# First attention layer: the scores of a pair of blocks in one call over four banks

## The chip, the cores and the metric

One core of one Trainium2 chip. The metric is device time in microseconds (us) of the whole kernel, the median of several runs.

## The reference, cut to what matters

```python
x = x + attn_a(layernorm(x))   # 16 heads of 8, blocks of 64 tokens, softmax inside a block
x = x + ffn(layernorm(x))      # top 2 of 8 experts
x = x + attn_b(layernorm(x))
x = x + ffn(layernorm(x))
# attn_a, per block of 64 tokens:
scores = einsum('bnihd,bnjhd->bnhij', q, k) / sqrt(8)
out = einsum('bnhij,bnjhd->bnihd', softmax(scores), v)
```

x has 16 rows of 256 tokens with 128 features, so 4096 tokens. Only the score step of attn_a is changed.

## The kernel before

The kernel runs six stages one after the other: setup, first layer, experts, second layer, experts, combine. In the first layer (`first_layer`) a tile is 128 tokens, a pair is two tiles (16 pairs), and a batch or quad, c, is four tiles (8 quads). Every engine runs its own written-out program over a common turn number p; semaphores counted by name tie them. A turn p of TensorE (PE) does: scores of pair p+1, the weighted sum over values of pair p-1 (`mixing`), transposes of the probabilities of pair p (`turn`), and the transpose back of pair p-1 (`flip`). Between them stand, in even turns, the projections K and Q of the next quad, the router's ranks and a transpose for the router (`turn_x2`); in odd turns the router's logits, the projection V and the transpose of the quad after next (`turn_x`).

The scores of a pair have two halves, gp 0 and 1. Half gp lies in `psS[gp]`, two PSUM banks of 512 columns. Within a half, `score(p, gp)` issues eight matmuls with 32 rows of K (one group of heads, g) and 64 columns of tokens, on tiles of the array given by `tile_position`. Matmuls in f32 leave two records each in the trace.

VectorE (DVE) does for each half `peak` (maximum over keys, L710) and `shift` (subtract it, L717, which writes `prob`), with `divide(p-2)` (L725, L729) between the two halves, and then in even turns the router's weights, places and statistics (from L791), in odd turns the router's choice (L737 to L767) and statistics. ScalarE (ACT) does `rise_up` (exponential, L880), `out_flat` (copies of the transposed probabilities, L886), `out_side` (L892), `out_k` (four copies, L857), `out_q` (L850), `out_v` (L867), the normalisation (L836) and, up to turn 6, the rounding of expert weights (`weight_high`, L900). GpSimd (POOL) adds the residual and sends rows to the experts' regions by indirect DMA (L479).

The waits that matter: `score(p, gp)` waits for `shifted` of the same half of pair p-1, since it overwrites it; `mixing(p-1)` waits for `divided` of pair p-2; `project_q` waits for `k_out`, since Q and K pass through one bank; `out_q(c)` waits for all scores that read the old `qT`; `project_v(c)` waits for `q_out` or, from the fourth quad on, for `taken`.

Of the kernel before, what the change touches and what calls it, by code (L numbers as in the profile page):

```python
# [330 lines left out]
def counted(k, tag, *names):  # L331

    return [k.sem(f"{tag}_{x}") for x in names]


def first_layer(k, d):

    nc = k.nc
    tag = "la"
    BLK = 64  # L340
# [3 lines left out]
    scored, peaked, shifted, risen, flat, flat_copied, mixed, mixed_copied, flipped, inverted, divided, based, summed = counted(  # L344
        k, tag, "scored", "peaked", "shifted", "risen", "flat", "flat_copied", "mixed", "mixed_copied", "flipped",
        "inverted", "divided", "based", "summed")
# [9 lines left out]
    psS = k.wide[0:2]  # L356
    psP, psO, psX = k.bank[4:6], k.bank[6], k.bank[7]
    with ExitStack() as ctx:
# [8 lines left out]
        xT, qT = two("xT", [P, TB]), sb("qT", [P, TB])  # L367
        kz = two("kz", [P, 4, TB])
# [137 lines left out]
        def _(pe):  # L506
# [10 lines left out]
            def project_k(c):  # L517
                pe.wait_ge(copied, c + 1)
                if c >= 4:
                    pe.wait_ge(spotted, c - 3)  # L520
                elif c >= 1:
                    pe.wait_ge(v_out, c)
                nc.tensor.matmul(psX[:, :], k.wqk[0][:, 1, :], xT[c % 2][:, :], start=True, stop=True).then_inc(k_ready, 1)

            def project_q(c):
                pe.wait_ge(k_out, c + 1)
                nc.tensor.matmul(psX[:, :], k.wqk[0][:, 0, :], xT[c % 2][:, :], start=True, stop=True).then_inc(q_ready, 1)

            def project_v(c):

                if c >= 3:
                    pe.wait_ge(taken, c - 2)
                else:
                    pe.wait_ge(q_out, c + 1)
                for tb in range(2 * BATCH):
                    for cls in range(2):
                        last = nc.tensor.matmul(
                            psX[BLK * cls:BLK * (cls + 1), tb * 64:(tb + 1) * 64], xT[c % 2][:, tb * BLK:(tb + 1) * BLK],
                            k.wv[0][:, cls * 64:(cls + 1) * 64], start=True, stop=True, tile_position=(0, BLK * cls))
                last.then_inc(v_ready, 1)  # L540
# [19 lines left out]
            def route_ranks(c):  # L560

                u = c % 2
                pe.wait_ge(picked, c + 1)
                if c + 3 < QUADS:
                    pe.wait_ge(v_out, c + 4)
                out = psX[:, 0:BATCH * EXPERTS].rearrange("p (t e) -> p t e", e=EXPERTS)
                wide = [P, BATCH, EXPERTS]
                nc.tensor.matmul(out, k.ones[:, :], k.region[:, :].unsqueeze(1).to_broadcast(wide), start=True, stop=False)
                nc.tensor.matmul(out, k.ones[:, :], both[u][:, BATCH, :].unsqueeze(1).to_broadcast(wide), start=False, stop=False)
                for t in range(BATCH - 1):  # L570
                    many = BATCH - 1 - t
                    nc.tensor.matmul(out[:, t + 1:, :], k.ones[:, :], both[u][:, t, :].unsqueeze(1).to_broadcast([P, many, EXPERTS]),
                                     start=False, stop=False)
                nc.tensor.matmul(out, k.upper[:, :], both[u][:, 0:BATCH, :], start=False, stop=True).then_inc(ranked, 1)

            def score(p, gp):
                c = p // 2
                if gp == 0 and p % 2 == 0:
                    pe.wait_ge(q_out, c + 1)
                if p >= 1:  # L580
                    pe.wait_ge(shifted, 2 * (p - 1) + gp + 1)
                for t in range(2):
                    for b in range(2):
                        at = slice((p % 2 * 2 + t) * P + b * BLK, (p % 2 * 2 + t) * P + (b + 1) * BLK)
                        for g2 in range(2):
                            g = 2 * gp + g2
                            last = nc.tensor.matmul(  # L587
                                psS[gp][BLK * b:BLK * (b + 1), g2 * 512 + t * 256:g2 * 512 + (t + 1) * 256],
                                qT[32 * g:32 * (g + 1), at], kz[c % 2][32 * g:32 * (g + 1), :, at],
                                start=True, stop=True, tile_position=(32 * g, BLK * b))  # L590
                last.then_inc(scored, 1)

            def turn(p, gp, w):
# [17 lines left out]
            def mixing(p):  # L611

                c = p // 2
                pe.wait_ge(flat_copied, 4 * p + 4)
                pe.wait_ge(v_out, c + 1)
                if p >= 1:
                    pe.wait_ge(divided, p)
                for t in range(2):
                    for gp in range(2):
                        for b in range(2):  # L620
                            for i in range(4):
                                col = t * 256 + gp * P + b * BLK
                                last = nc.tensor.matmul(
                                    psO[32 * i:32 * i + 2 * (HD + 1), col:col + BLK],
                                    stand[c % 2][:, p % 2 * 2 + t, b, 4 * gp + i, :],
                                    probT[p % 2][gp][t][:, i * P + b * BLK:i * P + (b + 1) * BLK], start=True, stop=True,
                                    tile_position=(0, 32 * i))
                last.then_inc(mixed, 1)

            def flip(p):  # L630
                pe.wait_ge(mixed_copied, p + 1)
                for x in range(4):
                    last = nc.tensor.transpose(psO[:, x * P:(x + 1) * P], side[:, x * P:(x + 1) * P], k.ident)
                last.then_inc(flipped, 1)

            for p in range(-3, 2 * QUADS + 6):
                c = p // 2
                even = p % 2 == 0
                here, ahead, behind = 0 <= p < PAIRS, 0 <= p + 1 < PAIRS, 0 <= p - 1 < PAIRS
                if ahead:  # L640
                    score(p + 1, 0)
                if even and 0 <= c - 3 < QUADS:
                    route_ranks(c - 3)
                if behind:
                    mixing(p - 1)
                if even and 0 <= c + 1 < QUADS:
                    project_k(c + 1)
                if not even and 0 <= c - 2 < QUADS:
                    route_logits(c - 2)
                if here:  # L650
                    turn(p, 0, 0)
                    turn(p, 0, 1)
                if ahead:
                    score(p + 1, 1)
                if behind:
                    flip(p - 1)
                if even and 0 <= c + 1 < QUADS:
                    project_q(c + 1)
                if not even and 0 <= c + 1 < QUADS:
                    project_v(c + 1)  # L660
                if here:
                    turn(p, 1, 0)
                    turn(p, 1, 1)
                if even and 0 <= c - 2 < QUADS:
                    turn_x2(c - 2)
                if not even and 0 <= c + 2 < QUADS:
                    turn_x(c + 2)
# [5 lines left out]
        def _(dve):  # L673
# [3 lines left out]
            for u in range(2):  # L677
                for cls in range(2):
                    last = nc.vector.memset(stand[u][BLK * cls:BLK * (cls + 1), :, :, :, cls * (HD + 1) + HD], 1.0)
# [26 lines left out]
                last.then_inc(moments2, 1)  # L706

            def peak(p, gp):
                dve.wait_ge(scored, 2 * p + gp + 1)
                nc.vector.tensor_reduce(most[gp][:, :], psS[gp][:, :].rearrange("p (h k) -> p h k", k=BLK), X, ALU.max)\  # L710
                    .then_inc(peaked, 1)

# [85 lines left out]
            for p in range(-4, 2 * QUADS + 6):  # L798
                c = p // 2
# [27 lines left out]
        def _(act):  # L827
# [18 lines left out]
            def out_q(c):  # L846
                act.wait_ge(q_ready, c + 1)
                if c >= 1:
                    act.wait_ge(scored, 4 * c)
                nc.scalar.activation(qT[:, :], psX, ACT.Identity, bias=k.cols[:, 0:1]).then_inc(q_out, 1)  # L850

            def out_k(c):
                act.wait_ge(k_ready, c + 1)
                if c >= 2:
                    act.wait_ge(scored, 4 * (c - 1))
                for j in range(4):
                    last = nc.scalar.activation(kz[c % 2][:, j, :], psX, ACT.Identity, bias=k.kbias[0][:, j:j + 1],  # L857
                                                scale=k.const[:, C_HEAD + j:C_HEAD + j + 1])
                last.then_inc(k_out, 1)
# [43 lines left out]
            for p in range(-4, 2 * QUADS + 6):  # L903
                c = p // 2
# [1039 lines left out]
```

## Time and profile before

| | |
|---|---|
| median of 3 runs | 886.98 us (883.74 to 887.29) |
| span of the profiled execution | 926.2 us |
| PE busy | 746.1 us, 81% |
| DVE busy | 505.9 us, 55% |
| ACT busy | 524.2 us, 57% |
| POOL busy | 363.0 us, 39% |
| mean granted TensorE clock | 0.902 |

The profiled execution is known by its span alone; it is 39 us longer than the median of the runs. The first layer fills the stretch from about 20 to 258 us. "Busy" counts an engine's own instructions; PE records of matmuls side by side overlap, so a busy PE is not a full array.

### The profile page before, as it was taken

What the parts mean: (1) busy time and instruction counts of PE and PEld (TensorE: products, weight loads), DVE (VectorE), ACT (ScalarE), POOL (GpSimd) and SP (SyncE); (2) the same over time, 40 slices, a digit from 0 to 9 for tenths busy, and PEclk for the clock granted to TensorE, in tenths of its full rate; (3) what the DMA queues carried; (4) which work ended last, traced back from release to release, by engine and by line L of the source; (5) the groups of instructions that cost most, each with busy time, mean ns of one, the idle gap of its engine ahead of it and who ended that gap; (6) DMA issues with size and microseconds to landing.
All of it is one profiled execution on the core that took longest, in us unless ns stands there. A gap on an engine that the chain in (4) does not pass through costs nothing. (4 is left out here: it accounts for less than half of the span.)

```text
span 926.2 us, 27043 instructions
## 1 busy us (share of the span) xinstructions
PE 746.1 (81%) x8818; PEld 600.2 (65%) x8819; DVE 505.9 (55%) x1787; ACT 524.2 (57%) x1016; POOL 363.0 (39%) x446
## 2 busy tenths in 40 slices
PE   1688887786179999999967898877629999999970
PEld 1356655455158888888834677666518888888860
DVE  3366876653435555555527565454435555555534
ACT  0589975652056666666617986643116666666630
POOL 0454764536713333333333114447642333333330
PEclk9989987885589999999999997997659999999985
DMA  6134011011211111111135000111121111111117
GB/s 193 38 98 121 22 40 36 25 31 56 75 39 48 46 46 46 49 49 46 38 107 172 11 4 24 30 33 41 40 72 40 48 49 47 46 46 46 49 33 268
DMA packets 53546, 54.45 MB, mean 59 GB/s; under 512 B 8192, under 2 KB 43008, under 8 KB 53472
## 3 DMA queue, kind: packets, MB, share of 16 engines
q1 hardware_dynamic: 41024, 31.61, 12.2%
q0 software_dynamic: 8640, 18.11, 6.0%
q10 hardware_dynamic: 3808, 3.70, 1.2%
q8 instruction: 53, 0.87, 0.4%
q14 instruction: 21, 0.17, 0.1%
HBM read 29.51 MB, written 23.86 MB: 58 GB/s over the span
## 5 line engine op out<-in xcount | busy, mean ns | idle before, releaser
L1656 POOL DMA_INDIRECT expert_out<-moe_b_out,moe_b_place x71 | 68.0, 957 | 145.3 <-DVE moe_b_out L1812 145.3
L1656 POOL DMA_INDIRECT expert_out<-moe_a_out,moe_a_place x71 | 68.0, 958 | 145.1 <-DVE moe_a_out L1812 145.1
L1688 PE MATMUL wide<-wgu,moe_b_hi 128*128 x284 | 94.9, 415 | 0.0
L1688 PE MATMUL wide<-wgu,moe_a_hi 128*128 x284 | 94.3, 413 | 0.0
L1069 POOL DMA_INDIRECT routed<-stream,lb_place x64 | 62.3, 974 | 63.1 <-PE wide L1117 18.5
L479 POOL DMA_INDIRECT routed<-stream,la_place x64 | 63.2, 987 | 42.9 <-DVE la_place L784 26.2
L1704 PE MATMUL wide<-wd,moe_a_hidT 128*128 x568 | 75.5, 276 | 1.4 <-DVE moe_a_out L1812 0.7
L1704 PE MATMUL wide<-wd,moe_b_hidT 128*128 x568 | 75.4, 276 | 1.3 <-DVE moe_b_out L1812 0.7
L1704 PEld LDWEIGHTS wide<-wd,moe_b_hidT 128*128 128x128 f32 x568 | 69.0, 192 | 2.2 <-issue 2.2
L1704 PEld LDWEIGHTS wide<-wd,moe_a_hidT 128*128 128x128 f32 x568 | 69.0, 192 | 2.2 <-issue 2.0
L1763 ACT ACTIVATE moe_b_glow<-wide 128x512 f32<-128x512 f32 x71 | 42.6, 599 | 44.1 <-PE wide L1688 44.0
L1763 ACT ACTIVATE moe_a_glow<-wide 128x512 f32<-128x512 f32 x71 | 42.5, 598 | 43.5 <-PE wide L1688 43.5
L1824 DVE TENSOR_TENSOR moe_b_hid<-wide,moe_b_glow 128x512 f32<-128x512 f32 x71 | 49.1, 692 | 20.7 <-PE wide L1688 9.2
L1824 DVE TENSOR_TENSOR moe_a_hid<-wide,moe_a_glow 128x512 f32<-128x512 f32 x71 | 49.1, 692 | 19.8 <-PE wide L1688 8.7
L1688 PE MATMUL wide<-wgu,moe_b_lo 128*128 x142 | 56.3, 396 | 0.0
L1688 PE MATMUL wide<-wgu,moe_a_lo 128*128 x142 | 56.0, 394 | 0.0
L1688 PEld LDWEIGHTS wide<-wgu,moe_b_hi 128*128 128x128 f32 x284 | 48.4, 190 | 6.9 <-issue 0.3
L1688 PEld LDWEIGHTS wide<-wgu,moe_a_hi 128*128 128x128 f32 x284 | 48.2, 190 | 6.5 <-issue 0.3
L1770 ACT ACTIVATE moe_b_hidT<-wide 128x512 f32<-128x512 f32 x71 | 42.4, 597 | 12.7 <-PE wide L1696 12.7
L1770 ACT ACTIVATE moe_a_hidT<-wide 128x512 f32<-128x512 f32 x71 | 42.4, 597 | 12.7 <-PE wide L1696 12.7
L710 DVE TENSOR_REDUCE la_most<-wide 128x16 f32<-128x1024 f32 x32 | 38.7, 1210 | 19.0 <-PE wide L587 18.9
L1812 DVE TENSOR_SCALAR moe_a_out<-wide,moe_a_weight 128x128 f32<-128x128 f32 x71 | 24.9, 351 | 39.4 <-PE wide L1704 39.4
(282 smaller groups left out, 1778.3 us busy)
## 6 DMA issues: line engine op xcount, KB each, us to landing
moe_a_rows<-routed SPq DMA_DIRECT2D x71, 67.0 KB
moe_b_rows<-routed SPq DMA_DIRECT2D x71, 67.0 KB
lb_outs<-expert_out SPq DMA_DIRECT2D x8, 512.0 KB
la_stage<-in_wg SPq DMA_DIRECT2D x8, 256.0 KB, 2.6
la_stage<-in_wu SPq DMA_DIRECT2D x8, 256.0 KB, 3.2
wd<-in_wd SPq DMA_DIRECT2D x8, 256.0 KB, 3.8
kept<-stream SPq DMA_DIRECT2D x8, 256.0 KB
lb_kept<-kept SPq DMA_DIRECT2D x8, 256.0 KB
```

The lines of the kernel that those rows point to most:

```text
L479: pool.indirect_dma_start(d.routed[:, :], bass.IndirectOffsetOnAxis(ap=place[:, t, j:j + 1], axis=0), k.stream[:, t, :], None).then_inc(se ...
L710: nc.vector.tensor_reduce(most[gp][:, :], psS[gp][:, :].rearrange("p (h k) -> p h k", k=BLK), X, ALU.max)\
L1069: pool.indirect_dma_start(d.routed[:, :], bass.IndirectOffsetOnAxis(ap=place[:, t, j:j + 1], axis=0), k.stream[:, t, :], None).then_inc(se ...
L1656: pool.indirect_dma_start(d.expert[:, :], bass.IndirectOffsetOnAxis(ap=place[s % 4][:, 0:1], axis=0), out[u][:, :], None).then_inc(stored[ ...
L1688: last = nc.tensor.matmul(ps[u][:, :], x[u][:, :], w(j, part), start=i == 0, stop=i == 2)
L1704: last = nc.tensor.matmul(psY[:, 0:D], hidT[u][:, c * P:(c + 1) * P], k.wd[:, bass.ds(e, 1), c, :].rearrange("p a c -> p (a c)"), start=c ...
L1763: nc.scalar.activation(glow[s % 2][:, :], psG[s % 2][:, :], ACT.Silu).then_inc(glowing.sem, 1)
L1770: nc.scalar.activation(hidT[u][:, :], psH[:, :], ACT.Copy).then_inc(crossed_copied.sem, 1)
L1812: nc.vector.tensor_scalar(out[u][:, :], psY[:, 0:D], weight[s % 4][:, 0:1], None, ALU.mult).then_inc(out_ready.sem, 1)
L1824: nc.vector.tensor_tensor(hid[u][:, :], psU[u][:, :], glow[u][:, :], ALU.mult).then_inc(hidden.sem, 1)
```

## The change

`score(p)` makes both halves at once: per tile and per 64 tokens it issues the four groups of heads one after the other, over both `psS[0]` and `psS[1]`. It waits for the second `shift` of pair p-1, signals `scored` once, and stands at one place in the turn: behind `flip` and the projection of Q or V, ahead of the second pair of `turn` calls. Before, half 0 stood at the head of the turn and half 1 ahead of `flip`. The waits on `scored` in `peak`, `out_q` and `out_k` are counted anew.

```diff
-            def score(p, gp):
+            def score(p):
                 c = p // 2
-                if gp == 0 and p % 2 == 0:
+                if p % 2 == 0:
                     pe.wait_ge(q_out, c + 1)
                 if p >= 1:
-                    pe.wait_ge(shifted, 2 * (p - 1) + gp + 1)
+                    pe.wait_ge(shifted, 2 * p)
                 for t in range(2):
                     for b in range(2):
...
-                        for g2 in range(2):
-                            g = 2 * gp + g2
-                            last = nc.tensor.matmul(
-                                psS[gp][BLK * b:BLK * (b + 1), g2 * 512 + t * 256:g2 * 512 + (t + 1) * 256],
+                        for g in range(4):
+                            col = g % 2 * 512 + t * 256
+                            last = nc.tensor.matmul(psS[g // 2][BLK * b:BLK * (b + 1), col:col + 256],
...
                 last.then_inc(scored, 1)
...
-                if ahead:
-                    score(p + 1, 0)
                 if even and 0 <= c - 3 < QUADS:
                     route_ranks(c - 3)
...
-                if ahead:
-                    score(p + 1, 1)
                 if behind:
                     flip(p - 1)
                 if even and 0 <= c + 1 < QUADS:
                     project_q(c + 1)
                 if not even and 0 <= c + 1 < QUADS:
                     project_v(c + 1)
+                if ahead:
+                    score(p + 1)
                 if here:
                     turn(p, 1, 0)
                     turn(p, 1, 1)
...
             def peak(p, gp):
-                dve.wait_ge(scored, 2 * p + gp + 1)
+                dve.wait_ge(scored, p + 1)
...
-                    act.wait_ge(scored, 4 * c)            # out_q
+                    act.wait_ge(scored, 2 * c)
...
-                    act.wait_ge(scored, 4 * (c - 1))      # out_k
+                    act.wait_ge(scored, 2 * (c - 1))
```

## Rows read from the trace of the kernel before

**Rows 1.** The page: span and busy time of the engines.
```profile
span 926.2 us, 27043 instructions
PE 746.1 (81%) x8818; PEld 600.2 (65%) x8819; DVE 505.9 (55%) x1787; ACT 524.2 (57%) x1016; POOL 363.0 (39%) x446
```

**Rows 2.** Busy time by stretch: length, PE, PEld, DVE, ACT, POOL, clock, DMA share, GB/s.
```profile
60.90:79.10 18.20, 15.36 (x273) 10.27 (x273) 13.53 (x30) 17.64 (x31) 9.87 (x14) 1.00 0.22 62
79.10:98.40 19.30, 16.73 (x285) 11.54 (x285) 12.27 (x43) 18.27 (x32) 8.50 (x14) 1.00 0.45 125
...
89.60:109.20 19.60, 17.03 (x294) 11.78 (x294) 15.28 (x51) 18.37 (x32) 10.12 (x13) 1.00 0.12 35
109.20:212.20 103.00, 81.87 (x1212) 55.83 (x1211) 65.70 (x194) 62.38 (x104) 56.52 (x76) 0.85 0.11 36
...
45.70:49.20 3.50, 1.18 (x6) 0.30 (x2) 3.43 (x4) 3.50 (x7) 3.42 (x4) 0.88 0.00 1
```

**Rows 3.** Timeline of PE: start, length, line, count, idle before and its releaser.
```profile
61.48 1.09 PE L587 MATMUL wide<-la_kz,la_qT 32*64 32x256 f32 x16
...
94.58 0.66 PE L633 MATMUL wide<-const,la_side 128*128 128x128 f32 x4
95.16 1.15 PE L537 MATMUL wide<-wv_a,la_xT 128*64 128x64 f32 x32
...
98.98 1.09 PE L587 MATMUL wide<-la_kz,la_qT 32*64 32x256 f32 x16
...
100.25 1.09 PE L623 MATMUL wide<-la_probT,la_stand 128*18 128x64 f32 x64
101.27 1.12 PE L523 MATMUL wide<-la_xT,wqk_a 128*128 128x512 f32 x2
102.23 1.04 PE L608 MATMUL wide<-const,la_prob 128*128 128x128 f32 x8
...
105.27 1.12 PE L527 MATMUL wide<-la_xT,wqk_a 128*128 128x512 f32 x2 [0.39 <-ACT la_kz L857]
...
109.18 1.09 PE L587 MATMUL wide<-la_kz,la_qT 32*64 32x256 f32 x16
```

**Rows 4.** Timeline of ACT, the same columns, 90 to 105 us.
```profile
90.20 1.05 ACT L880 ACTIVATE la_prob<-la_prob 128x1024 f32<-128x1024 f32 x1
...
92.68 1.14 ACT L900 ACTIVATE wgu<-la_stage 128x512 fp32r<-128x512 f32 x2
93.72 0.58 ACT L892 ACTIVATE la_side<-wide 128x512 f32<-128x512 f32 x1
...
102.43 2.78 ACT L857 ACTIVATE la_kz<-wide,kbias_a,const 128x512 f32<-128x512 f32 x4 [0.21 <-PE wide L523]
```

**Rows 5.** Timeline of DVE, the same columns, 62 to 100 us.
```profile
62.64 1.23 DVE L710 TENSOR_REDUCE la_most<-wide 128x16 f32<-128x1024 f32 x1 [0.45 <-PE wide L587]
...
92.73 0.19 DVE L737 TENSOR_TENSOR la_logit<-wide,stream 128x32 f32<-128x32 f32 x1 [4.20 <-PE wide L556]
...
96.48 1.19 DVE L710 TENSOR_REDUCE la_most<-wide 128x16 f32<-128x1024 f32 x1
97.70 1.23 DVE L717 TENSOR_TENSOR la_prob<-wide,la_most 128x1024 f32<-128x1024 f32 x1
98.84 0.35 DVE L725 RECIPROCAL la_inv<-wide 128x32 f32<-128x32 f32 x1
99.22 0.42 DVE L729 TENSOR_TENSOR la_mix<-wide,la_inv 128x256 f32<-128x256 f32 x1
```

**Rows 6.** Timeline of PE in the second layer: one of its score calls.
```profile
590.75 1.13 PE L1181 MATMUL wide<-lb_kz,lb_qT 32*32 32x128 f32 x64
```

**Rows 7.** Timelines of PE and ACT in the slower stretch, 120 to 144 us.
```profile
120.12 1.98 PE L587 MATMUL wide<-la_kz,la_qT 32*64 32x256 f32 x16
...
133.11 1.09 PE L587 MATMUL wide<-la_kz,la_qT 32*64 32x256 f32 x16
...
143.55 1.27 ACT L867 ACTIVATE la_stand<-wide 64x512 f32<-64x512 f32 x2 [4.78 <-remote]
```

More of the change, by code:

```diff
@@ L584, in score @@
                         at = slice((p % 2 * 2 + t) * P + b * BLK, (p % 2 * 2 + t) * P + (b + 1) * BLK)
-                        for g2 in range(2):
-                            g = 2 * gp + g2
-                            last = nc.tensor.matmul(
-                                psS[gp][BLK * b:BLK * (b + 1), g2 * 512 + t * 256:g2 * 512 + (t + 1) * 256],
-                                qT[32 * g:32 * (g + 1), at], kz[c % 2][32 * g:32 * (g + 1), :, at],
-                                start=True, stop=True, tile_position=(32 * g, BLK * b))
+                        for g in range(4):
+                            col = g % 2 * 512 + t * 256
+                            last = nc.tensor.matmul(psS[g // 2][BLK * b:BLK * (b + 1), col:col + 256],
+                                                    qT[32 * g:32 * (g + 1), at], kz[c % 2][32 * g:32 * (g + 1), :, at],
+                                                    start=True, stop=True, tile_position=(32 * g, BLK * b))
                 last.then_inc(scored, 1)
```

## The prediction

> **What bounds the kernel now.** I read the page first, to see that no engine is full over the whole span: PE is busy 81%, ACT 57%, DVE 55% [rows 1]. The change touches the first layer alone, so I went to the busy times by stretch. There the reader is to see that two regimes exist. From 60.9 to 109.2 us the TensorE clock is granted in full, and one batch of four blocks (two pairs, an even and an odd turn of the loop) takes 18.2 us without routing, 19.3 when routing begins and 19.6 with all of it. PE works 15.4 to 17.0 us of that, ACT 17.6 to 18.4, DVE 12 to 15 [rows 2]. Nobody idles much, and nobody is full: the period is a chain of hand-overs between engines, with PE and ACT both close to it. From 109.2 to 212.2 the same work takes 103 us at a mean clock of 0.85 [rows 2]; that is four more batches and part of a fifth, some 26 us each.
>
> Third, PE's timeline. In an even turn it starts the next pair's first half of scores at 98.98, mixing at 100.25, K at 101.27, Q only at 105.27 (idle 0.39, for ACT), and the next odd turn starts at 109.18: 10.20 us [rows 3]. Fourth and fifth, the timelines of ACT and DVE, for the durations and hand-overs below [rows 4, 5].
>
> **What the old order gives.** The scores of a pair lie in two halves, psS[0] and psS[1]. PE makes half 0 of pair p+1 at the head of turn p, and half 1 in its middle, each released by its own subtraction on DVE. So DVE works on half 0 of the next pair long before PE comes to that pair's turn, and the division of pair p-2, which DVE does after that half, is done when PE reaches mixing(p-1), which waits for it: DVE starts its division at 98.84 and the product at 99.22, PE mixes at 100.25 after other work [rows 3, 5].
>
> **What the change removes.** A call for one half is eight matmuls of 256 columns, in 16 records; two calls make a pair. A call's records span 1.09 us at full clock, of which the next work overlaps some 0.07: it holds PE 1.02 [rows 3]. The new call has 16 matmuls, 32 records. The trace has no such call, so I bound it: below 1.09, as if eight matmuls ran side by side at the price of four; above 2.04, two old calls. The nearest row is the second layer's scores, L1181, where 64 records of 128 columns on eight tiles take 1.13 us: twice the column-records of an old half in the same time [rows 6]. I take 1.05. The saving is 1 us of PE per pair, 16 us over 16 pairs, if PE were alone.
>
> The Trainium skill, "TensorE: Matmul & The Clock Gate", section "The mechanism" of its part on packing, says that a weight load overlaps running matmuls only where its row group differs. The loads of the second half-block share all four row groups with running matmuls; by that rule a call would cost near 2.04. The row of L1181, where four column groups share each row group, speaks against it.
>
> **What it adds.** Three things. The whole score(p+1) now waits for the second subtraction of pair p; it stands behind mixing, K or router logits, turn(p,0), flip and Q or V on PE; and DVE's first maximum of pair p+1 waits for it. So the head start is gone, and DVE and PE are tied into a loop once per turn. I walk that loop from the start of the first maximum of a pair to that of the next.
>
> Even turn. Maximum 1.22, subtraction to the division's start 1.14 (96.48 to 98.84 is 2.36), reciprocal 0.38, product 0.42, hand-over 0.06 (K copies end at 105.21, Q starts 105.27): mixing starts at 3.22. Mixing 1.02 (100.25 to 101.27); K to its copies 1.16 (101.27 to 102.43); copies to Q 2.84 (102.43 to 105.27); Q holds PE 0.96 (as K, 101.27 to 102.23); score to DVE's start 1.16 (61.48 to 62.64) [rows 3, 4, 5]. Sum 3.22 + 1.02 + 1.16 + 2.84 + 0.96 + 1.16 = 10.36 us. The second subtraction ends at about 5.5, hidden. DVE's own work (5.52 and some 2 of weighing and statistics) is hidden too.
>
> Odd turn, while ACT still rounds weights (turns up to 6). The subtraction ends 1.22 + 1.23 + 0.06 = 2.51; ACT does the exponential, four normalisations and two weight copies in 3.52 (90.20 to 93.72); side copy and hand-over 0.64; flip 0.58 (94.58 to 95.16); V 1.15; score to DVE 1.16 [rows 3, 4, 5]: 9.56 us. Without weights ACT gives back 1.04 (92.68 to 93.72) and the chain is 8.52, but DVE then sets the end: 2.36 + 0.80 + 2.36 for both halves and the division, and 3.75 for routing and statistics (92.73 to 96.48): 9.27 us [rows 4, 5]. V's own wait for the routed logits is inside that.
>
> Side effects at no cost: out_q(c+1) now waits for the score behind Q (before, both halves were issued ahead of it). ACT gets to it at the end of its second exponential anyway, about 10.1, and the score ends at 10.4; behind it stand two copies of turned probabilities, which need PE's turns after that score. They end at about 12.1 of the even turn and the next mixing is due at 13.6: 1.5 of slack. The copy for the router behind them ends near the next exponential's due time, so that cover is thin; if it goes, 0.5 us per batch. No DMA moves; POOL's residual keeps its place behind the division.
>
> **The sum.** Batches of two turns, new against old: turns 2 and 3, 10.36 + 9.56 = 19.92 against 18.2, +1.7; turns 4 and 5, 19.92 against 19.3, +0.6; turns 6 on, 10.36 + 9.27 = 19.63 against 19.6, nothing, for five batches [rows 2]. At the start V(0) now stands ahead of score(0): 1.15 later, less a little caught up; +1.0. Together +3.3, say 3.5 with rounding of hand-overs. The tail (turns 15 on) has no scores, and POOL's row writes follow the routing, which shifts with it.
>
> The profiled execution spans 926.2 us, 39 more than the median 886.98. In it V of turn 9 should take 1.15 us, but ACT gets its result at 143.55 after 4.8 us idle [rows 7], and the clock falls afterwards. I take these stalls to be mostly absent from the timed runs: four to five batches at 26 instead of 19.6 are about the 39. So against the profile's own time: 926.2 + 3.5 = 929.7; against the median 886.98 + 3.5 = 890.5. About 0.5% (4.4 us) is what a measurement can tell from no change.
>
> **Rivals.**
> - *The clock falls more often* (0.2). In an even turn PE, once flip is done at about 6.9, waits for K's copies until 8.26: 1.4 us idle, and about 1.2 before mixing. For it: the stretch 45.7 to 49.2, with PE busy 1.18 of 3.5 and the clock still 0.88, is where it goes to half [rows 2]. Against it: here PE would be busy some 7.3 of 10.4 us. Price: at half clock a score call takes 1.98 instead of 1.09 [rows 3, 7]; mixing, K, Q and score on the chain cost 3.5 more per even turn. Eight times 3 is +24: 914; if half of them, 902.
> - *PE is what counts, and it is faster* (0.16). In the slow regime two calls of 1.98 stand on PE's path, and the old even turn from 120.12 to 133.11 takes 13.0 us [rows 7]. With mixing and K at half clock (about 1.9 and 2.1) and the rest at full, my chain is 3.22 + 1.9 + 2.1 + 2.84 + 0.96 + 1.16 = 12.2, so 0.8 less, and odd turns with the stall save the like. If the timed runs have these stretches, four or five batches give back 1.7 each, 8 in all, and a stall avoided 3.7: 887 + 3.5 - 8 - 3.7 = 879. It decides from three slow batches on. Against it: the 39 us.
> - *The eight don't run side by side* (0.06), the call costs 2.04: +1.0 in each of 15 turns: 905.5. This is also the case in which the change does not do what it says.
> - *Thin covers go* (0.11): the router copy, V's wait, ACT behind out_q: 0.5 to 1 us per batch, 894 to 898.
> - *My forecast* (0.47): 890.5, own range 886 to 895.
>
> **How the numbers follow.** The likeliest is 890.5. The range takes most of both rivals on the slow side up to 905 and the faster one down to 880. Slower by over 0.5% (above 891.4): the clock 0.2, no side by side 0.06, thin covers 0.09 and 0.1 of my own case, 0.45. Faster (below 882.5) 0.15. Within: 0.40.
>
> **What would show it.** After: L587 calls of x32 with about 1.1 us; DVE idle before the first maximum of odd turns, 2 to 3 us, released by PE L587 (about none before); L623 waiting for DVE's product (L727 in the new numbering, L729 now) in nearly every turn, where it did so in few; Q waiting about 1.4 us for ACT's K copies; the batch at 60 to 80 us 19.9 instead of 18.2. Wrong if DVE has no such idle time, or if PEclk has more low slices than before.

## The result, and the profile after

The changed kernel takes 893.59 us (median of 15 runs, 888.58 to 905.65), the kernel before 886.64 beside it (15 runs). The ratio is 1.0085, with a 95% interval of 1.0061 to 1.0109: 7.5 us slower, 5.4 to 9.7 (the medians differ by 7.0). The forecast was 890.5, 3.5 slower: the time lies in the forecast range, the loss is twice the one forecast.

The profiled execution of the changed kernel took 890.17 us, so it can be read against its own runs. The one of before that stands ahead of the prediction cannot: its stalls, some 39 us of late results and low clock, are missing here. The page, with the tenths of busy time and of clock in 40 slices, and the group of DVE's first-layer maxima, last the same group of the kernel before:

```profile
span 887.9 us, 27043 instructions
PE 704.6 (79%) x8818; PEld 578.7 (65%) x8819; DVE 503.4 (57%) x1787; ACT 525.5 (59%) x1016; POOL 363.5 (41%) x446
...
PE   1466677774199999999977889997269999999960
...
PEclk9989999986599999999998999997579999999995
...
L708 DVE TENSOR_REDUCE la_most<-wide 128x16 f32<-128x1024 f32 x32 | 39.1, 1220 | 57.6 <-PE wide L588 57.5
```

```profile
L710 DVE TENSOR_REDUCE la_most<-wide 128x16 f32<-128x1024 f32 x32 | 38.7, 1210 | 19.0 <-PE wide L587 18.9
```

DVE works as much as before (503.4 against 505.9 us [rows 1]) and now idles 57.6 us ahead of its 32 maxima, all but 0.1 of it for the score call; before it was 19.0. That is the lost head start. Lines of the new kernel: score L588, mixing L623, K L523, Q L527, V L537, turned probabilities L608.

Timeline of PE: the end of an odd turn that still has the expert weights on ACT, an even turn, and the mixings that close the next odd one (start, length, line, count, idle before and its releaser), to be laid beside [rows 3]:

```profile
65.01 1.09 PE L623 MATMUL wide<-la_probT,la_stand 128*18 128x64 f32 x64 [1.47 <-DVE la_mix L727]
...
79.00 0.66 PE L633 MATMUL wide<-const,la_side 128*128 128x128 f32 x4 [1.22 <-ACT la_side L890]
79.59 1.15 PE L537 MATMUL wide<-wv_a,la_xT 128*64 128x64 f32 x32
80.67 1.12 PE L588 MATMUL wide<-la_kz,la_qT 32*64 32x256 f32 x32
...
85.25 1.09 PE L623 MATMUL wide<-la_probT,la_stand 128*18 128x64 f32 x64 [1.47 <-DVE la_mix L727]
86.27 1.13 PE L523 MATMUL wide<-la_xT,wqk_a 128*128 128x512 f32 x2
...
88.10 0.60 PE L633 MATMUL wide<-const,la_side 128*128 128x128 f32 x4
90.27 1.12 PE L527 MATMUL wide<-la_xT,wqk_a 128*128 128x512 f32 x2 [1.57 <-ACT la_kz L855]
91.33 1.12 PE L588 MATMUL wide<-la_kz,la_qT 32*64 32x256 f32 x32
92.38 1.09 PE L608 MATMUL wide<-const,la_prob 128*128 128x128 f32 x8
...
95.91 1.09 PE L623 MATMUL wide<-la_probT,la_stand 128*18 128x64 f32 x64 [1.34 <-DVE la_mix L727]
...
105.50 1.09 PE L623 MATMUL wide<-la_probT,la_stand 128*18 128x64 f32 x64 [1.32 <-DVE la_mix L727]
```

Timelines of DVE and ACT over the same two turns, beside [rows 4, 5]:

```profile
72.31 1.23 DVE L708 TENSOR_REDUCE la_most<-wide 128x16 f32<-128x1024 f32 x1 [3.87 <-PE wide L588]
...
81.90 1.23 DVE L708 TENSOR_REDUCE la_most<-wide 128x16 f32<-128x1024 f32 x1 [2.80 <-PE wide L588]
...
84.68 0.42 DVE L727 TENSOR_TENSOR la_mix<-wide,la_inv 128x256 f32<-128x256 f32 x1
...
92.55 1.22 DVE L708 TENSOR_REDUCE la_most<-wide 128x16 f32<-128x1024 f32 x1 [3.87 <-PE wide L588]
```

```profile
74.83 1.06 ACT L878 ACTIVATE la_prob<-la_prob 128x1024 f32<-128x1024 f32 x1 [0.80 <-DVE la_prob L715]
...
78.38 0.57 ACT L890 ACTIVATE la_side<-wide 128x512 f32<-128x512 f32 x1
...
87.43 2.79 ACT L855 ACTIVATE la_kz<-wide,kbias_a,const 128x512 f32<-128x512 f32 x4 [0.43 <-PE wide L523]
```

The loop of the even turn can be read off: first maximum 81.90, product 84.68, mixing 85.25, K 86.27, copies 87.43, Q 90.27, score 91.33, next first maximum 92.55. Every step comes behind the one named ahead of it, four times on another engine. It took 10.65 us. The loop of the odd turn before it took 9.59: first maximum 72.31, exponential 74.83, side copy 78.38, flip 79.00, V 79.59, score 80.67, next first maximum 81.90. The odd turn after it, from mixing 95.91 to 105.50, took 9.59 as well.

Busy time by stretch (length, PE, PEld, DVE, ACT, POOL, clock, DMA share, GB/s):

```profile
60.00:100.00 40.00, 27.43 (x546) 19.72 (x543) 27.20 (x65) 35.72 (x61) 18.53 (x25) 1.00 0.35 95
100.00:200.00 100.00, 75.69 (x1433) 57.84 (x1432) 77.03 (x229) 76.85 (x127) 65.72 (x87) 0.93 0.14 44
139.00:143.00 4.00, 4.00 (x35) 3.67 (x37) 3.83 (x27) 2.87 (x5) 3.21 (x3) 0.57 0.29 87
```

From 60 to 100 us the clock is full and PE is busy 27 of 40 us, with 17 of 20 in [rows 2] before. Then come low stretches, a few microseconds at about half clock, as at 139 (0.57 over 4 us); they fall into turns 8, 9 and 13. Over 100 to 200 us the clock is 0.93.

### The profile page after: what moved, and what is told of

Same layout as the page of the kernel before. It is cut to its first block and busy times, and to the rows that moved or that the text cites. A ratio compares the mean times of both kernels' runs of the same rounds, so it can differ in the third digit from the quotient of the medians.

```text
span 887.9 us, 27043 instructions
## 1 busy us (share of the span) xinstructions
PE 704.6 (79%) x8818; PEld 578.7 (65%) x8819; DVE 503.4 (57%) x1787; ACT 525.5 (59%) x1016; POOL 363.5 (41%) x446
## 5 line engine op out<-in xcount | busy, mean ns | idle before, releaser
L708 DVE TENSOR_REDUCE la_most<-wide 128x16 f32<-128x1024 f32 x32 | 39.1, 1220 | 57.6 <-PE wide L588 57.5
```

## The experiments

The runs form four groups, each on a chip of its own. On all four chips the kernel before took 935 to 940 us, not 887, so each ratio is to the kernel before on the same chip. Only kernels of one group ran beside each other; across groups only the ratios can be set side by side, and with care, since the change itself costs more on some chips than on others. Each turn length below comes from one profiled execution and goes from the start of one mixing to the start of the next.

**Chip 1 (before: 934.69).** Is the stall of the first profile a matter of that execution? The kernel before, unchanged.

> The kernel before, unchanged, profiled once more. If the 4.8 us stalls of V in the first profile belong to that one execution, its span now is near 885 us, ACT waits for V about 0.2 us per turn, and four late batches take about 19.6 us each. If they belong to the kernel, the span is again over 915. Clock theory (the change costs time because the clock falls more often): this profile has fewer low stretches between 60 and 200 us than the changed kernel's, which has five. Lost head start: the same number, within one.

936.76 us, ratio 1.0011 [0.9971, 1.0051]. Timeline of ACT: V's result of turn 9 is late again, as in [rows 7]:

```profile
143.50 1.27 ACT L867 ACTIVATE la_stand<-wide 64x512 f32<-64x512 f32 x2 [4.84 <-remote]
```

The stalls, results of PE that reach ACT some microseconds late, recur at the same place and size, and they are in the timed runs: 35 of them have a median of 934.69. So "mostly absent from the timed runs" holds for the chip of the result, where the profile of the changed kernel has none either, and not because one execution had bad luck. On which chip the first profile was taken isn't on record.

Then the two parts of the change apart. First the place alone, on the kernel before: the old calls of eight, one behind the other at the new place.

```diff
-                if ahead:
-                    score(p + 1, 0)
...
-                if ahead:
-                    score(p + 1, 1)
...
                     project_v(c + 1)
+                if ahead:
+                    score(p + 1, 0)
+                    score(p + 1, 1)
```

> Position alone: the two old calls of eight matmuls, each with its own wait and signal, both at the new place. Lost head start (the place costs, the merging does nothing): 893 to 896 us, the same as the changed kernel within 0.3%, even turns again 10.5 us. Rival, the merged call itself costs (one signal for both halves, sixteen matmuls ahead of the second transposes): 886 to 889, back at before.

942.91 us, 1.0073 [1.0035, 1.0112]. Timeline of PE in an even turn:

```profile
69.86 1.12 PE L527 MATMUL wide<-la_xT,wqk_a 128*128 128x512 f32 x2 [1.57 <-ACT la_kz L856]
70.92 1.15 PE L587 MATMUL wide<-la_kz,la_qT 32*64 32x256 f32 x32
```

Two calls next to each other run side by side without being merged, 32 records in 1.15 us (merged 1.12), and the wait ahead of Q is the same 1.57. Here the even turns are 10.6 us too. So the place alone brings the long even turn and a loss, and merging at that place saves 0.03 us per pair. What merging does to the whole time isn't settled: the merged call was not run on this chip, and on chip 2 it has 1.0161 [1.0112, 1.0211] (e5 below). The intervals touch, and a cost of merging of some microseconds where results come late is not excluded.

Now the opposite, on the changed kernel: the merged call in a better place, ahead of `flip` and of Q or V.

```diff
+                if ahead:
+                    score(p + 1)
                 if behind:
                     flip(p - 1)
...
-                if ahead:
-                    score(p + 1)
```

> Merging kept, place moved: score(p+1) stands ahead of flip and of Q or V, right behind the first transposes. Lost head start through K, its copies and Q: the even loop is freed of 3.9 us and DVE sets it, late batches 17 to 17.7 us instead of 20, total 870 to 879 us. If the wait for the second subtraction alone is what costs, 890 to 894. Clock theory: no forecast below 884, since PE idles no less.

926.8 us, 0.9888 [0.9851, 0.9925]: faster than the kernel before, and than e2 beside it. The pair's scores need only Q and K of their own batch, which are ready; the call no longer stands behind K's copies. Timeline of PE:

```profile
59.97 1.12 PE L523 MATMUL wide<-la_xT,wqk_a 128*128 128x512 f32 x2
...
61.90 1.12 PE L588 MATMUL wide<-la_kz,la_qT 32*64 32x256 f32 x32
...
64.86 1.12 PE L527 MATMUL wide<-la_xT,wqk_a 128*128 128x512 f32 x2 [1.25 <-ACT la_kz L855]
66.78 1.86 PE L608 MATMUL wide<-const,la_prob 128*128 128x128 f32 x8 [0.80 <-ACT la_prob L878]
69.32 1.55 PE L623 MATMUL wide<-la_probT,la_stand 128*18 128x64 f32 x64 [0.69 <-ACT la_probT L884]
```

The wait for K's copies stays, but nothing on DVE waits behind it. The next chain, by the releasers in these rows, is ACT's: copies of K, exponential, copies of turned probabilities. Its two batches ahead of the stalls (turns 2 and 3, 4 and 5) take 18.75 and 19.26 us rather than the 17 to 17.7 that I had written: right in sign, too hopeful in the size of a batch (the total, 0.9888 of 887, would be 877, within 870 to 879). (Turn 2, the last rows above, has a low stretch in it.)

The same place in even turns alone (`if ahead and even`), the new place in odd ones:

> As the last, but only in even turns (ahead of flip and Q); in odd turns the score stays behind V. Theory of the K to Q chain: most of the gain comes here, late batches 17.7 to 18.7 us, total 875 to 883. If odd turns matter as much, only half of the gain of the last run.

937.37 us, 0.9994 [0.9954, 1.0034]: no gain over the kernel before, against both of my forecasts. Up to turn 7 the even turns take 8.8 to 9.7 us and the odd ones behind them 11.8 to 13.2: the time is given back in the next turn, where `flip` waits for ACT's side copy (1.90 us at 74.81, 1.77 at 96.29) and V behind it runs at low clock (1.98 us for 1.15). Against the changed kernel's 1.0161 on chip 2 it still is 1.6% better.

**Chip 2 (before: 936.67).** The changed kernel unchanged, on a chip with the stalls.

> The changed kernel, unchanged, beside before on this chip. Lost head start: even turns 10.65 us at full clock again, ratio to before 1.005 to 1.012. Where the stalls of V and mixing are present on the chip (before near 935), they hit this kernel as well and the ratio stays within that.

949.23 us (6 runs), 1.0161 [1.0112, 1.0211]: 15 us by the ratio, 12.6 by the medians, against 7.5 and 7.0 on the chip of the result. It lies above the 1.005 to 1.012 that I had written. The even turns up to 4 take the loop's 10.66 us, those from turn 6 on 12.5. Against e1's profile turns 1 to 5 are 7.1 us longer and turns 6 to 13 5.3 longer.

Next, the first term of the loop. On the changed kernel, the division of pair p-2 goes ahead of the first maximum, so that mixing needn't wait for it:

```diff
+                if 0 <= p - 2 < PAIRS:
+                    divide(p - 2)
                 if p < PAIRS:
                     peak(p, 0)
...
-                if 0 <= p - 2 < PAIRS:
-                    divide(p - 2)
```

> Changed kernel with one edit: on DVE the division of pair p-2 goes ahead of the first maximum of pair p, into the time in which DVE waits for the scores. Theory: in even turns mixing waits for maximum, subtraction and division (3.35 us after the scores), and with them K, its copies, Q and the next score. With the division done early mixing starts 1.3 to 1.5 us sooner: even turns 9.2 to 9.4 us, odd turns unchanged, total 8 to 12 us (0.9 to 1.3%) below the changed kernel, ratio to before 0.995 to 1.000. Rival (the chain runs over something else, such as ACT's exponential or the clock): no more than 3 us below the changed kernel.

943.08 us, 1.008 [1.0049, 1.0111]: 6 us better than the changed kernel by the medians, short of the 8 to 12 that I had written. The even turns, from mixing to mixing, took 11.5. But mixing itself has moved, so the loop is read from maximum to maximum as above. Timelines of DVE, PE and ACT:

```profile
83.29 1.22 DVE L708 TENSOR_REDUCE la_most<-wide 128x16 f32<-128x1024 f32 x1 [1.39 <-PE wide L588]
...
94.10 1.23 DVE L708 TENSOR_REDUCE la_most<-wide 128x16 f32<-128x1024 f32 x1 [4.05 <-PE wide L588]
```

```profile
85.10 1.09 PE L623 MATMUL wide<-la_probT,la_stand 128*18 128x64 f32 x64
...
91.11 1.12 PE L527 MATMUL wide<-la_xT,wqk_a 128*128 128x512 f32 x2 [2.02 <-ACT la_kz L855]
92.17 1.88 PE L588 MATMUL wide<-la_kz,la_qT 32*64 32x256 f32 x32
```

```profile
85.80 1.06 ACT L878 ACTIVATE la_prob<-la_prob 128x1024 f32<-128x1024 f32 x1
...
88.28 2.77 ACT L855 ACTIVATE la_kz<-wide,kbias_a,const 128x512 f32<-128x512 f32 x4
```

Mixing no longer waits, K is made earlier, but in ACT's program the exponential, weights and the side copy stand ahead of K's copies. They start at 88.28 without idle time, and Q waits 2.02. From the first maximum, mixing starts 1.81 us later rather than 3.35, but the score only 8.88 rather than 9.43: of 1.54 us gained on DVE's side, ACT's order leaves 0.55. The score call then runs at low clock (1.88), and the loop from 83.29 to 94.10 takes 10.81 us for 10.65. The gain in time doesn't lie in this loop: turns 6 to 13, those with late results, take 98.6 us for 106.3 in e5's profile. Why they are shorter isn't shown.

The better place in odd turns alone (`if ahead and not even`):

> The merged call ahead of flip and V in odd turns alone; in even turns it stays behind Q. Theory: odd turns were set by DVE or by ACT's normalisation and copies as much as by V, so this gains little: 0 to 4 us below the changed kernel. If the odd turns carry the loss, 6 us or more below it.

941.59 us, 1.0074 [1.0046, 1.0102]: 8 us below the changed kernel, where I had written 0 to 4, and 6 or more if the odd turns carry the loss. In its profile turns 2 to 5, at the start, are no shorter (43.8 us for 41.5 in e5); the gain lies in turns 6 to 13 (101.9 for 106.3) and ahead of turn 2.

Both improvements together (place in all turns, division first):

> Both repairs: merged call ahead of flip in all turns, division ahead of the first maximum. The merged call ahead of flip alone took 18.9 us per batch, set in even turns by K, four copies, copies of probabilities, exponential, transposes. The division is no part of that chain, so 0 to 3 us below that version: ratio to before 0.985 to 0.989.

929.86 us, 0.9917 [0.9885, 0.995], above the 0.985 to 0.989 that I had written. No gain over the place alone (0.9888 on chip 1); the intervals overlap. Turn 2 takes 9.65 us here and 9.64 in e11 below, which has the place alone: once the score stands early, the division's place is worth nothing there.

**Chip 3 (before: 939.68).** To see the loop without stalls: three kernels in which POOL sends all rows to the experts' regions behind its loop, 64 lots, rather than in the turns. The computation is the same.

```diff
-                    for t in range((c - 3) * BATCH, (c - 3) * BATCH + 2):
-                        if 0 <= t < TILES:
-                            dispatch(t)
...
+            for t in range(TILES):
+                dispatch(t)
```

> Before, with one edit: POOL sends the 64 lots of rows of the first layer by indirect DMA only after its loop over the turns. Theory on the stalls: V and mixing stall where they run beside these DMAs. Then V is never waited for by 4.8 us, late batches take 19.6 us at a full clock, the last turn with scores is near 188 us instead of 208, and the whole is some 25 to 35 us longer, since 81 us of row writes now follow the loop. If the stalls have another cause, late batches stay at 26 us and the whole is 50 us longer.

966.57 us, 1.0261 [1.0211, 1.0311]: longer by 27, as the rows now go when nothing covers them. And the stalls are gone: from turn 4 to 12 the turns take 9.95 or 9.96 and 9.62 to 9.65 us, every time. So on this chip the first layer's stalls need POOL's indirect row transfers beside its matmuls; whether it is POOL's issuing or the transfers themselves isn't told apart. (The edit leaves the second layer's rows where they were, and that layer is as slow as on the other chips, see below.) On the chip of the result they don't come even so: timelines of the changed kernel there, V's result taken at once while rows go out:

```profile
119.53 1.15 PE L537 MATMUL wide<-wv_a,la_xT 128*64 128x64 f32 x32
```

```profile
120.72 1.28 ACT L865 ACTIVATE la_stand<-wide 64x512 f32<-64x512 f32 x2
```

```profile
120.43 1.11 POOL L479 DMA_INDIRECT routed<-stream,la_place  x1 [0.17 <-issue]
```

> The changed kernel with the same edit. This is the change without the stalls. Against the last run: my sum says +3.5 us; with the even turns at 10.65 instead of 10.36 and a start 2 us later than I had, +7 to +8. If the stalls made most of the loss seen on this chip (12.6 us), the difference here is 8 or less; if it stays at 12, the loss is all in the order of the turn.

978.11 us, 1.0402 [1.0352, 1.0452]: 11.5 more than e9, with no stall in either's first layer. That is near the 12 for which I had written that the loss is all in the order of the turn, and far from the 3.5 of my sum. Busy time by stretch, e9 first, then e10 with a low stretch of its own:

```profile
100.00:200.00 100.00, 82.86 (x1470) 59.23 (x1462) 81.61 (x274) 76.81 (x130) 29.46 (x51) 0.98 0.06 18
```

```profile
100.00:200.00 100.00, 75.77 (x1450) 58.58 (x1448) 78.67 (x252) 78.61 (x131) 29.16 (x50) 0.95 0.07 21
...
100.00:104.00 4.00, 4.00 (x72) 3.19 (x70) 2.55 (x21) 3.03 (x6) 1.25 (x4) 0.66 0.47 134
```

Timelines of PE, the mixing of turn 14 in e9, and then in e10 together with turn 5, whose V (L533) runs at low clock, 1.71 us:

```profile
178.71 1.09 PE L619 MATMUL wide<-la_probT,la_stand 128*18 128x64 f32 x64
```

```profile
97.10 1.09 PE L619 MATMUL wide<-la_probT,la_stand 128*18 128x64 f32 x64 [1.35 <-DVE la_mix L723]
...
101.49 1.71 PE L533 MATMUL wide<-wv_a,la_xT 128*64 128x64 f32 x32
...
189.63 1.09 PE L619 MATMUL wide<-la_probT,la_stand 128*18 128x64 f32 x64 [2.30 <-DVE la_mix L723]
```

By turn 14 the changed order is 10.9 us behind, turn by turn accounted for below. Read in windows of 0.5 us from 40 us on, e10 has low stretches from about 48, 58, 99, 140 and 181 us, e9 ahead of 190 us only one, from 49 to 56.5 (longer than one of e10's).

> The merged call ahead of flip in all turns, with the same edit. Batches of 18.9 instead of 19.6 us, and no loss at turns 2 to 6: 6 to 12 us below the first run of this call.

963.01 us, 1.0229 [1.0181, 1.0278]: 3.6 below e9, with overlapping intervals, where I had written 6 to 12. In the first layer the better place does give that: mixing of turn 14 at 170.13 against 178.71. Of these 8.6 us 5.0 are left when POOL begins with the rows (197.57 against 202.57): a low stretch, e11's only one from 40 to 184 us, falls into turn 14, which takes 8.25 us for 6.81, and the rest behind the last score runs at low clock from 185 us on, in e9 from 196.

**Chip 4 (before: 937.05).** Does the low clock come from PE's wait for K's copies? e10's kernel, with four matmuls of 512 bf16 columns in the gap ahead of Q in even turns, whose results nobody uses:

```diff
+                if even and here and ahead:
+                    pe.wait_ge(shifted, 2 * (p + 1))
+                    for _ in range(4):
+                        nc.tensor.matmul(psS[0][:, 0:512].rearrange("p (t c) -> p t c", c=P), k.ones[:, :],
+                                         k.ones[:, :].unsqueeze(1).to_broadcast([P, 4, P]), start=True, stop=True)
                 if even and 0 <= c + 1 < QUADS:
                     project_q(c + 1)
```

> The changed kernel with row writes last, and in each even turn four extra matmuls of 512 bf16 columns in the 1.57 us in which PE idles ahead of Q (into a score bank that the next score overwrites; they wait for the second subtraction of the pair). Their results are not used. Theory of the clock term: the odd turns of 10.6 us, against 9.0 for the others, come from low stretches of 3.4 us that follow this idle time. Then all odd turns from turn 7 on take 9.0 to 9.1, no low stretch lies between 60 and 190 us, and the median is 3 to 5 us below the same kernel without them (978.1, ratio to before 1.040), so near 1.035 to 1.037. If the odd turns stay at 10.6 in places, the low clock has another cause.

982.58 us, 1.0493 [1.0466, 1.0519]; I had written 3 to 5 us faster than e10, a ratio of 1.035 to 1.037. Timeline of PE, then busy time over the low stretch behind it (columns as above):

```profile
89.33 1.03 PE L652 MATMUL wide<-ones 128*128 128x512 bf16 x4
91.06 1.13 PE L523 MATMUL wide<-la_xT,wqk_a 128*128 128x512 f32 x2 [0.70 <-ACT la_kz L856]
...
98.07 1.88 PE L552 MATMUL wide<-wr,la_x2T 128*128 128x8 f32 x8
```

```profile
97.00:104.50 7.50, 7.50 (x116) 6.91 (x112) 5.02 (x28) 5.20 (x11) 2.55 (x5) 0.54 0.40 113
```

The gap is filled to 0.70 and the clock falls nonetheless, a turn later, to 0.54 over 7.5 us. Turns 5 and 13 grow to 12.19 us, while the three odd ones between them stay at 9.03 (in e10 one of these, turn 9, took 10.61). The gap ahead of Q alone is not what lowers the clock.

## Why the prediction was right, and where its sizes were off

The range held the time, and the mechanism that the prediction named is the one that the runs show. The size of the loss was right only to a factor of two, and part of the closeness of 890.5 to 893.6 is luck, as the last paragraphs here say.

**The new call's price: right.** It was taken at 1.05 us and holds PE from 91.33 to 92.38, 1.05; its records span 1.12. Neither "the eight don't run side by side" nor "PE is what counts, and it is faster" came about: with PE's time 1 us per pair shorter the kernel is slower, and on a chip with the slow batches, where that rival was to gain, it loses 1.6% (e5).

**The loop: right.** Each link is in the rows above. Measured against forecast, even turn: to mixing 3.35 (3.22), mixing 1.02 (1.02), K to copies 1.16 (1.16), copies to Q 2.84 (2.84), Q to score 1.06 (0.96), score to DVE 1.22 (1.16); 10.65 for 10.36. Odd turn with weights: to the exponential 2.52 (2.51), ACT's work to the side copy 3.55 (3.52), side copy to flip 0.62 (0.64), flip 0.59 (0.58), V 1.08 (1.15), score to DVE 1.23 (1.16); 9.59 for 9.56. Without weights and low clock 9.03 to 9.17 for 9.27. The 0.64 was the copy and a hand-over of 0.06; the old rows have 0.86 there (93.72 to 94.58), and the new kernel shows that the smaller value was the right one. The signs that the prediction named are there: DVE idle before a first maximum (3.87 in odd turns, where 2 to 3 was named, and 2.80 in an even one), mixing released by the product in 14 of 16 turns, one before, Q waiting 1.57 (1.4), the batch from 65.01 to 85.25 20.24 us (19.92). e2 shows that the place does this, and e3 and e11 that a place ahead of K's copies undoes it: e11's even turns take 8.93 to 9.81 us at full clock.

**The sum: too small.** e9 and e10 have both orders without stalls. Starts of consecutive mixings differ, in us:

| turns | forecast | e10 less e9 | of it |
|---|---|---|---|
| start and turn 1 | +1.0 | +3.1 | 12.57 for 9.81 in turn 1, start 0.3 later |
| 2, 3 | +1.7 | +2.1 | 10.66 for 8.99, 9.58 for 9.19 |
| 4, 5 | +0.6 | +1.7 | turn 5 10.61 for 9.63 |
| 6, 7 | 0 | +0.1 | 10.66 for 9.96, 9.04 for 9.62 |
| 8, 9 | 0 | +1.7 | turn 9 10.61 for 9.64 |
| 10, 11 | 0 | +0.1 | 10.66 for 9.95, 9.03 for 9.65 |
| 12, 13 | 0 | +2.2 | turn 13 10.61 for 9.10 |

The sum is 10.9. Where the clock stays up, a late batch costs 0.1 (forecast: nothing): the even turn loses 0.7 and the odd one gives 0.6 back. Three terms were mis-sized. The even turn by 0.3, six times, 1.8 us: the hand-overs at Q and at the score took 0.16 more together, the way to mixing 0.13. The start by 2.1: in e10 a second low stretch falls into turn 1, which the changed kernel on the chip of the result did in 10.47 us. And the odd turns 5, 9 and 13, where a low stretch costs 1.0, 1.6 and 1.6 us: 4.2. Four odd turns without weights take 0.24 less each than forecast, and the old turn 13 is 0.5 shorter than its fellows: 3.3 + 1.8 + 2.1 + 4.2 - 1.0 + 0.5 is the 10.9.

The changed kernel's profile on the chip of the result says the same. Its turns 2 to 13, from mixing 65.01 to mixing 189.08, take 124.1 us where the forecast has 118.4. The 5.7 more are 1.8 of the even turns, 4.7 of the low stretches in turns 8, 9 and 13 (12.14, 10.63 and 10.63 us), less 0.8 of shorter odd turns.

So the term that failed most is the clock, which my own case put at nothing. The rival "the clock falls more often" was partly true, and is the larger part of what was missing. From 56.5 to 190 us e9 has no low stretch, e10 four and e11, with the better place, one, in one profile each. Its place was wrong and its price too high: in e10 no even turn ran at half clock (10.65 or 10.66 throughout); stretches in some odd turns did, and one in turn 8 of the changed kernel's profile (12.14). It was priced at +24 or +12 on top.

**The stalls.** "These stalls mostly absent from the timed runs" gave the right base, 887, for the wrong reason (e1): that is luck. On the chip of e5 the change costs 12.6 to 15 us. Nor are the 39 us four or five batches of the first layer. The second layer has its share, though nothing in it was changed. All its PE transposes of probabilities, in the changed kernel on the chip of the result and then in e5 (ns least, median, most; first and last start in us):

```profile
L1209 PE MATMUL wide<-const,lb_prob x128: 272/273/476, 488.1 to 603.7; 128*128 128x128 f32 x128
```

```profile
L1209 PE MATMUL wide<-const,lb_prob x128: 272/273/476, 518.2 to 657.3; 128*128 128x128 f32 x128
```

They take 115.6 us here and 139.1 there; in the first profile 140.0 (504.4 to 644.4), in e9, with the first layer's rows moved, still 142.1. So the first profile's excess lies about half in each layer: 24.4 us in the second, by the changed kernel's 115.6, and 22.8 in the first, by e9 (mixing of turn 14 at 201.46 against 178.71). Measured against two different kernels, the two don't add up to the 39 exactly.

**Open.** The result has 7.5, e10 less e9 11.5 in the medians. (The two profiled executions differ by only 6.0 although the rows begin 10.8 later: the unchanged second layer took 3.9 less in e10, 138.2 for 142.1.) The kernel before was not profiled on the chip of the result, so whether it has fewer low stretches of its own there isn't known. Nor is it known what starts a low stretch in an odd turn; the late place brings more of them, e12 excludes the gap ahead of Q as the sole cause. "Thin covers go" can't be told apart: `out_q` waited 0.48 for the score, but e10's even turns keep the loop's length to 0.01 us.

## What to carry to other kernels

Ask of a merged call what head start its halves had: the time of the call (1 us of PE per pair saved here) is small beside a consumer that now starts only when all of it is done. Two adjacent calls on tiles that don't overlap ran side by side anyway (1.15 us for 1.12), so merging buys little there and the place decides: a call belongs where its inputs are ready and ahead of a chain that it doesn't need (0.9888 of the time before, against 1.0161 behind that chain, on two chips with late results). Before an engine's wait is shortened, look at what the next in-order engine of the loop has ahead of it (e6: of 1.54 us, 0.55 arrived).

A time close to the forecast isn't yet a sum that holds: compare the loss with the forecast loss, turn by turn.

## What was unexpected of the hardware

- The same program takes 887 us on one chip and 935 to 940 on four others. The difference lies about equally in the two attention layers. In the first, V's results reach ACT up to 4.8 us late, and ACT waits up to 7.7 us for a result of the mixing (e1); the profile gives these waits no releasing engine, only "remote". Without row transfers in these turns they are gone (e9), and turns of a kind agree to 0.03 us. Why one chip is spared isn't known.
- 32 score records take 1.12 us in one call and 1.15 as two adjacent calls, 16 alone 1.09.
- The clock falls to about half for a few microseconds in a kernel whose PE waits are 1.3 to 2.3 us each, several per turn (e10, 0.66 over 100 to 104 us); filling one of them with 1.03 us of matmuls did not keep it up (e12, 0.54 over 97 to 104.5).
